# A macaron transformer in float32 on one core: the expert layers as two halves of 648 columns, with LoRA amid the next tile's product

## The chip, the cores and the metric

The kernel runs on one core of a Trainium2 chip. Its engines are TensorE (PE in the profile; its weight loads are PEld), VectorE (DVE), ScalarE (ACT), GpSimd (POOL) and SyncE (SP), which issues the DMAs. Each executes its own instructions in order and waits on semaphores for the others. The time is that of one execution on the device, in microseconds; the lower the better.

## The reference

```python
x = L0_attn_x                                    # [2, 1024, 512] float32
x = x + 0.5 * L0_ffn(layernorm(x))               # weight-normed W + lora_B @ lora_A
x = x + L0_attn(layernorm(x))                    # 32 heads of 16, 8 kv heads, rope, causal
x = x + 0.5 * L0_ffn(layernorm(x))
x = x + 0.5 * L1_ffn(layernorm(x))               # experts
x = x + L1_attn(layernorm(x))                    # 8 heads of 32, causal
x = x + 0.5 * L1_ffn(layernorm(x))
...
def L1_ffn(x, W_base, b_base, W_router, lora_A, lora_B):       # E = 8 experts, R = 16, top 2
    logits = xf @ W_router.T                                   # [tokens, 8]
    topk_p, topk_i = top_k(softmax(logits), 2)
    topk_p = topk_p / sum(topk_p)
    w = sum(one_hot(topk_i, 8) * topk_p[..., None], axis=1)
    h = einsum('td,erd->ter', xf, lora_A)                      # [tokens, 8, 16]
    lora_out = einsum('ter,eor,te->to', h, lora_B, w) * 2.0
    return x @ W_base.T + b_base + lora_out
```

## The kernel before, in words

Each of the two sequences (1024 rows of 512) goes through eight stages, numbered FFN_A, QKV0, WO0, FFN_B, MOE_A, QKV1, WO1, MOE_B. MOE_A and MOE_B are the expert layers. A stage works on eight tiles of 128 rows. Stages are joined to three chains, [FFN_A, QKV0], [WO0, FFN_B, MOE_A, QKV1] and [WO1, MOE_B], with an attention after each of the first two. In a chain a list of (stage, tile) items is run through in software-pipelined steps: at step i every engine does its share of item i, i-1, i-2 and so on. The order within a step is written out by hand, once per engine, in the function `chain` of that engine; semaphores do the rest.

For an item, GpSimd computes the inverse deviation (`rstd_of`, L1191 and L1193), VectorE the statistics (`statistics`, L803, L805) and the normalised tile xn (`normalise`, L815), TensorE transposes it into a bank called `turn` (`turn_x`, L567), ScalarE copies the high part out of it (`copy_turned`, L1051), VectorE subtracts that to get the low part (`turned_lo`, L822), and TensorE multiplies (`product`): a float32 product is made of three passes in a rounded format, high x high, high x low and low x high (`three_passes`, L587, L588, L589), over four chunks of 128 input features. The result stands in one of two pairs of PSUM banks, `prod[n % 2]`, and VectorE takes it up (`epilogue`: L847 or L850 for x, L841 for QKV). Weights of the next stage are split into high and low parts during tiles 2 to 5 of the stage before, one chunk a tile, the high part on ScalarE (L1060), the low part on GpSimd (`split_chunk`, L1184). GpSimd also adds the bias to x ahead of the update (`bias_x`, L1204).

An expert item has more. TensorE's `router` multiplies the tile by `whl`, the 128 columns of all experts' lora_A and the 8 columns of the router, 136 columns into bank 1 of the pair. VectorE's `routing` takes the two greatest logits and their places and forms two rows of gates (L864 to L873), with an exponential on ScalarE (L1066) between; each of the nine steps waits for the one before (`link`). `weigh` adds the rows (L877) and multiplies the 128 columns by them (L881, to `hw`). TensorE transposes hw (`turn_hw`, L617), ScalarE copies it out (`copy_hw`, L1071), and TensorE adds its product with lora_B to bank 0, where the base product of 512 columns stands (`lora`, L622). The bias is halved once at the start and the update multiplies the product by 0.5.

TensorE's step i is: transposes of item i, turn_hw of item i-2, router of item i-1, lora of item i-2, base product of item i-1. VectorE's is: statistics of item i+2, normalise i+1, low part of i, update of i-2, routing and weighing of i-1.

## Time and profile before

| | before |
|---|---|
| median of 3 runs | 1426.17 us |
| all three | 1425.89, 1426.17, 1436.26 us |
| the profiled execution | 1425.2 us, span of its instructions 1423.5 us |
| TensorE busy | 1298.5 us, 91% of the span, 7328 matmuls |
| VectorE busy | 963.8 us, 68%, 2846 instructions |
| ScalarE, GpSimd busy | 630.8 us (44%), 485.5 us (34%) |
| chain that ended last | PE 68%, DVE 17%, POOL 5%, issue 5%, ACT 3%, DMA 2% |
| DMA | 38.50 MB, mean 27 GB/s |

Busy times come from the profile of one execution. Matmuls overlap in it (a record lasts until the results are out), so a TensorE that is busy by the profile need not be issuing at its full rate; the time from one matmul's start to the next one's tells its cost. The clock column gives the share of full speed that TensorE was granted.

### The profile page before, as it was taken

The page shows a single profiled execution, that of the slowest core. Times are in us where ns is not written, and L with a number is a line of the kernel's source. Part 1 is how long each engine was busy: PE and PEld are TensorE (multiplying, and loading weights), DVE is VectorE, ACT ScalarE, POOL GpSimd, SP SyncE. Part 2 cuts the span into 40 slices and gives each one's busy share as a digit, 9 for nine tenths or more (in the row PEclk, how much of TensorE's full clock was granted, in tenths as well). Part 3 has the DMA queues.
Part 4 walks back from the last instruction along what each step waited for, and adds up shares of the span by engine and source line. Part 5 has one row for each costly group of instructions (what it writes and reads, how often), then busy time and mean ns, then how long its engine had stood idle before and what let it go on. Part 6 is the DMA issues. An engine that isn't in the chain of part 4 may idle for free.

```text
span 1423.5 us, 21475 instructions
## 1 busy us (share of the span) xinstructions
PE 1298.5 (91%) x7328; PEld 799.1 (56%) x7328; DVE 963.8 (68%) x2846; ACT 630.8 (44%) x929; POOL 485.5 (34%) x734
## 2 busy tenths in 40 slices
PE   4997999999899898998879889999988999999898
PEld 1875544444277686445658754444434877854366
DVE  5765898899257845644758467999871787376276
ACT  1245366666622245443212544766665222634421
POOL 1574032221255442116426621311223653311261
PEclk8999599999999998999989975999999999989999
DMA  9200000110011000000130000010100100000001
GB/s 299 88 1 30 2 2 2 32 32 3 1 35 37 1 1 30 2 1 5 55 144 1 24 8 2 3 32 2 32 3 1 56 15 1 31 2 2 1 16 45
DMA packets 19932, 38.50 MB, mean 27 GB/s; under 512 B 4416, under 2 KB 6208, under 8 KB 19712
## 3 DMA queue, kind: packets, MB, share of 16 engines
q1 hardware_dynamic: 19824, 37.12, 7.8%
q8 instruction: 60, 0.98, 0.3%
q14 instruction: 48, 0.39, 0.1%
HBM read 31.21 MB, written 11.01 MB: 30 GB/s over the span
## 4 chain that ended last, share of the span: by engine, by line
PE 68%; DVE 17%; POOL 5%; issue 5%; ACT 3%; DMA 2%; SPq 0%; DVEq 0%; ACTq 0%; POOLq 0%
PE bank L758 15%; PE bank L660 12%; PE bank L587 7%; PE bank L589 7%; PE bank L588 7%; DVE maxes L949 5%; PE bank L742 4%; PE bank L640 4%; PE bank L736 3%; DVE unused L945 3%; PE bank L567 2%; PE bank L622 2%; PE bank L670 2%; POOL probs L1221 2%; DVE x L847 1%
## 5 line engine op out<-in xcount | busy, mean ns | idle before, releaser
L1149 ACT ACTIVATE probs<-bank 128x1024 f32<-128x1024 f32 (+3 forms) x416 | 368.0, 911 | 301.5 <-PE bank L742 192.5
L660 PE MATMUL bank<-ops 48*128 48x512 f32 (+3 forms) x960 | 323.5, 441 | 13.3 <-DVE maxes L949 4.1
L945 DVE CUSTOM_DVE_ANT_0 unused<-bank,causal 128x128 bf16<-128x128 f32 (+3 forms) x640 | 279.4, 486 | 73.0 <-PE bank L660 69.8
L1301 POOL TENSOR_SCALAR_AFFINE_SELECT probs<-probs 128x256 f32<-128x256 f32 (+1 forms) x256 | 118.8, 464 | 587.6 <-ACT probs L1149 587.3
L660 PEld LDWEIGHTS bank<-ops 48*128 48x128 f32 (+1 forms) x960 | 164.2, 208 | 198.1 <-DVE maxes L945 79.6
L758 PE MATMUL bank<-probs,v_mem 128*17 128x512 f32 (+6 forms) x1920 | 256.1, 524 | 6.1 <-ACT heads_raw L1138 5.6
L949 DVE TENSOR_REDUCE maxes<-bank 128x1 f32<-128x512 f32 x320 | 207.3, 684 | 40.3 <-PE bank L660 38.8
L1051 ACT CAST xT<-bank 128x512 fp32r<-128x512 f32 (+1 forms) x128 | 71.2, 560 | 271.7 <-PE bank L567 271.7
L742 PE MATMUL bank<-ops 50*128 50x512 f32 (+2 forms) x640 | 178.5, 454 | 4.9 <-ACT probs L1149 4.8
L822 DVE TENSOR_TENSOR xT<-bank,xT 128x512 fp32r<-128x512 f32 (+1 forms) x128 | 83.5, 655 | 125.0 <-ACT xT L1051 124.9
L587 PE MATMUL bank<-w_odd_hi,xT 128*128 128x512 f32 (+1 forms) x384 | 155.4, 405 | 1.9 <-DVE xT L822 1.9
L589 PE MATMUL bank<-w_odd_hi,xT 128*128 128x512 f32 (+1 forms) x384 | 138.0, 359 | 0.0
L588 PE MATMUL bank<-w_odd_lo,xT 128*128 128x512 f32 (+1 forms) x384 | 137.7, 359 | 0.0
L742 PEld LDWEIGHTS bank<-ops 50*128 50x128 f32 x640 | 88.0, 200 | 58.2 <-ACT probs L1149 29.7
L1106 ACT CAST ops<-bank 128x512 fp32r<-128x512 f32 x144 | 81.7, 587 | 65.9 <-PE bank L640 65.7
L587 PE MATMUL bank<-ops,xT 128*128 128x512 f32 x224 | 100.3, 448 | 4.0 <-DVE x L847 1.6
L640 PE MATMUL bank<-identf,features 128*128 128x128 f32 x512 | 78.5, 290 | 19.5 <-POOL heads_raw L1258 13.9
L1191 POOL TENSOR_SCALAR var_eps<-mv 128x1 f32<-128x1 f32 x96 | 38.9, 405 | 159.1 <-DVE mv L805 158.9
L589 PE MATMUL bank<-ops,xT 128*128 128x512 f32 x224 | 90.1, 402 | 0.0
L588 PE MATMUL bank<-ops,xT 128*128 128x512 f32 x224 | 89.8, 401 | 0.0
L758 PEld LDWEIGHTS bank<-probs,v_mem 128*17 128x17 f32 (+1 forms) x1920 | 41.0, 99 | 78.0 <-issue 52.6
L640 PEld LDWEIGHTS bank<-identf,features 128*128 128x128 f32 x512 | 62.4, 147 | 37.7 <-POOL heads_raw L1258 17.3
(109 smaller groups left out, 1896.1 us busy)
## 6 DMA issues: line engine op xcount, KB each, us to landing
w_odd_lo<-staging_wqkv SPq DMA_DIRECT2D x4, 1536.0 KB, 6.7
x<-x_dram SPq DMA_DIRECT2D x16, 256.0 KB, 5.9
out_dram<-x SPq DMA_DIRECT2D x16, 256.0 KB, 2.0
staging_wqkv<-wqkv_dram SPq DMA_DIRECT2D x2, 1536.0 KB, 14.0
ops<-staging_dora SPq DMA_DIRECT2D x3, 1024.0 KB, 5.5
ops<-shiftT SPq DMA_DIRECT2D x160, 4.0 KB
w_odd_lo<-staging_wo SPq DMA_DIRECT2D x2, 1024.0 KB, 5.2
ops<-staging_base SPq DMA_DIRECT2D x2, 1024.0 KB, 5.5
```

What stands on the lines that cost most here:

```text
L587: mm(dst, x_hi[:, k, :], hi[:, k, :], start=(k == 0), stop=False)
L588: mm(dst, x_hi[:, k, :], lo[:, k, :], start=False, stop=False)
L589: last = mm(dst, x_lo[:, k, :], hi[:, k, :], start=False, stop=(k == kc - 1 and not lora))
L640: last = nc.tensor.transpose(dst[:, k * P:(k + 1) * P], src, identf[:])
L660: last = mm(dst[:, h * w:(h + 1) * w], queries(a, u)[rows, t // 4, hi, t % 4 * P:(t % 4 + 1) * P], keys(a, u, hi)[rows, HALF * kp:HALF * k ...
L742: last = mm(dst, keys(a, u, 0)[rows, block], queries(a, u)[rows, c, heads_of[0]:heads_of[-1] + 1, columns], start=True, stop=True)
L758: last = mm(heads[a.head_rows * h:a.head_rows * h + a.dim + 1, q0 - HALF * c:HALF], v[:, j, a.kv_head(u, r, i), :], probs[:, e % 6, n, fir ...
L822: V.tensor_tensor(xT[:, n % 2, 1, 0:kc, :], turn[n % 2][:, 0:kc * P].rearrange("p (k c) -> p k c", k=kc), xT[:, n % 2, 0, 0:kc, :].bitcast ...
L945: V.tensor_tensor_reduce(unused[:, masked % 3, 0:w], part, causal[:, HALF - w:], 1.0, NEG, ALU.add, ALU.max, dst).then_inc(s["max_done"].s ...
L949: V.tensor_reduce(dst, part, AX.X, ALU.max).then_inc(s["max_done"].sem, 1)
L1149: A.activation(probs[:, e % 6, :, 0:cols], scores[:, 2 * (e % 2):2 * (e % 2) + 2, 0:cols], ACT.Exp, scale=a.scale).then_inc(s["exp"].sem, 1)
L1301: G.affine_select(out=p, in_=p, compare_op=ALU.is_ge, fill=0.0, base=0, pattern=pattern, channel_multiplier=-1).then_inc(s["masked"].sem, 1)
```

## The change

The expert layers' three weight matrices (lora_A, router, base: 128 + 8 + 512 columns) become one of 648 columns, staged, loaded and split together. Each tile's product is done as two halves of 324 columns: the first holds lora_A, the router and the first 188 columns of the base, the second the other 324 columns of the base. turn_hw of the tile before comes between the halves, writing to a `turn` bank, and lora of the tile before after the second chunk of the second half; it is now two matmuls, into 188 columns of bank 1 and 324 of bank 0. The 188 base columns of the first half are added to x in `routing`, and the update has two parts. Routing is shorter: ScalarE takes the exponential of the difference of the two greatest logits by itself and copies the places, and the division by the sum moves into the weighing multiply. On VectorE the low part now comes first in every step of every chain, routing before normalise, and weighing stays last. QKV's 768 columns are multiplied as 384 + 384, before 512 + 256. The region X grows, and the base weights are loaded after unit 6 of the first attention, before after unit 5.

```diff
-        whl = sb("whl", [P, 2, KC, ER + EXPERTS], F32R)
-                   "X": [ops_flat[:, 4096:6144], ops_flat[:, 6144:8192]],
+                   "X": [ops_flat[:, 4096:7168], ops_flat[:, 7168:10240]],
...
-                    if st == QKV0 and u in (3, 5):
+                    if st == QKV0 and u in (3, 6):
...
+                st3, t3 = divmod(n - 3, NT)
+                if st3 in MOE_RANK:
+
+                    pe.wait_ge(hwT_ready.sem, hwT_ready.at(b, MOE_RANK[st3] * NT + t3 + 1))
...
-                for c in range(2 if st in ATT else 1):
-                    cols = slice(c * 512, min(hi.shape[2], (c + 1) * 512))
...
+                w = hi.shape[2] // (2 if st in ATT else 1)
+                for c in range(hi.shape[2] // w):
+                    cols = slice(c * w, (c + 1) * w)
+                    last = three_passes(prod[n % 2][:, c, 0:w], n, hi[:, :, cols], lo[:, :, cols], between=between)
+                last.then_inc(prod_ready.sem, 1)
+
+            def expert_half(b, st, t, first, between=None):
+
+                n = begin(b, st, t) if first else st * NT + t
+                if t == 0 and first:
+                    pe.wait_ge(w_ready.sem, w_ready.at(b, chunks_before(st + 1)))
+                cols = slice(0, MOE_HALF) if first else slice(MOE_HALF, MOE_COLS)
+                last = three_passes(prod[n % 2][:, 1 if first else 0, 0:MOE_HALF], n, weights(st, 0)[:, :, cols],
+                                    weights(st, 1)[:, :, cols], lora=not first, between=between)
+                if first:
+                    last.then_inc(hl_ready.sem, 1)
...
-                mm(prod[n % 2][:, 0, :], hwT[r % 2], wlora[:, :], start=False, stop=True).then_inc(prod_ready.sem, 1)
+                mm(prod[n % 2][:, 1, MOE_HALF:MOE_HALF + BASE_FIRST], hwT[r % 2], wlora[:, 0:BASE_FIRST], start=True, stop=True)
+                mm(prod[n % 2][:, 0, 0:MOE_HALF], hwT[r % 2], wlora[:, BASE_FIRST:], start=False, stop=True
+                   ).then_inc(prod_ready.sem, 1)
...
+                    if st in MOE_RANK:
+                        first, rest = x[:, t, 0:BASE_FIRST], x[:, t, BASE_FIRST:]
+                        dve.wait_ge(base_added.sem, base_added.at(b, MOE_RANK[st] * NT + t + 1))
+                        V.scalar_tensor_tensor(first, prod[n % 2][:, 1, MOE_HALF:MOE_HALF + BASE_FIRST], 0.5, first,
+                                               ALU.mult, ALU.add)
+                        V.scalar_tensor_tensor(rest, prod[n % 2][:, 0, 0:MOE_HALF], 0.5, rest, ALU.mult, ALU.add
+                                               ).then_inc(x_new.sem, 1)
...
+                V.max(top[:], logits).then_inc(route_top.sem, 1)
+                dve.wait_ge(route_top.sem, route_top.at(b, r + 1))
+                V.max_index(top_at[:], top[:], logits).then_inc(route_at.sem, 1)
+                dve.wait_ge(x_biased.sem, x_biased.at(b, BIAS_RANK[st] * NT + t + 1))
+                V.scalar_tensor_tensor(x[:, t, 0:BASE_FIRST], prod[n % 2][:, 1, ER + EXPERTS:MOE_HALF], 0.5,
+                                       x[:, t, 0:BASE_FIRST], ALU.mult, ALU.add).then_inc(base_added.sem, 1)
...
+                dve.wait_ge(route_exp.sem, route_exp.at(b, 2 * (r + 1)))
+                V.tensor_scalar(route[:, 1:2], route[:, 0:1], 1.0, 0.5, ALU.add, ALU.mult).then_inc(route_sum.sem, 1)
+                V.tensor_scalar(gate[:, 1, :], expert_no[:], top_atf[:, 1:2], route[:, 0:1], ALU.is_equal, ALU.mult
+                                ).then_inc(route_second.sem, 1)
+                dve.wait_ge(route_sum.sem, route_sum.at(b, r + 1))
+                V.reciprocal(route[:, 2:3], route[:, 1:2]).then_inc(route_inv.sem, 1)
+                dve.wait_ge(route_second.sem, route_second.at(b, r + 1))
+                V.scalar_tensor_tensor(gate[:, 0, :], expert_no[:], top_atf[:, 0:1], gate[:, 1, :], ALU.is_equal, ALU.add
+                                       ).then_inc(gate_sum.sem, 1)
...
             def chain(b, its):
                 for i in range(len(its) + 4):
+                    if i < len(its):
+                        turned_lo(b, *its[i])
                     if i + 2 < len(its):
                         statistics(b, *its[i + 2])
+                    experts = 1 <= i < len(its) + 1 and its[i - 1][0] in MOE_RANK
+                    if experts:
+                        routing(b, *its[i - 1])
                     if i + 1 < len(its):
                         normalise(b, *its[i + 1])
-                    if i < len(its):
-                        turned_lo(b, *its[i])
...
-                act.wait_ge(route_step.sem, route_step.at(b, 9 * r + 2))
-                A.activation(route[:, 1:2], route[:, 0:1], ACT.Exp).then_inc(route_exp.sem, 1)
+                act.wait_ge(route_top.sem, route_top.at(b, r + 1))
+                A.activation(route[:, 0:1], top[:, 0:1], ACT.Exp, bias=top[:, 1:2], scale=-1.0).then_inc(route_exp.sem, 1)
+                act.wait_ge(route_at.sem, route_at.at(b, r + 1))
+                A.copy(top_atf[:], top_at[:, 0:2]).then_inc(route_exp.sem, 1)
```

VectorE in the middle of MOE_A, before. A row is a line of the kernel, the operation, what it writes and reads, its partitions x elements, and the semaphores that it waits for. `top` and `top_at` are the greatest logits and their places, `gate` the gates, `hw_mem` the weighed activations.

```order
L803 BN_STATS stats<-x 128x6 [waits x_new]
L805 BN_AGGR mv<-stats 128x2 [waits ln_stat]
L815 TENSOR_SCALAR probs<-x,mv,rstd 128x512 [waits turned,ln_rstd]
L822 TENSOR_TENSOR xT<-bank,xT 128x512 [waits xT_hi_ready]
L847 SCALAR_TENSOR_TENSOR x<-bank,x 128x512 [waits x_biased,prod_ready]
L864 MAX top<-bank 128x8 [waits hl_ready]
L865 TENSOR_TENSOR route<-top 128x1 [waits route_step]
L866 MAX_INDEX top_at<-top,bank 128x8 [waits route_step]
L867 CAST top_atf<-top_at 128x2 [waits route_step]
```

The same place now (the kernel's lines have other numbers: L844 is the low part, L837 normalise, L887 to L891 routing, L872 and L874 the update, L898 to L910 weighing):

```order
L904 SCALAR_TENSOR_TENSOR gate<-expert_no,top_atf,gate 128x8 [waits route_second]
L910 SCALAR_TENSOR_TENSOR hw_mem<-bank,route,gate 128x128 [waits gate_sum,route_inv]
L844 TENSOR_TENSOR xT<-bank,xT 128x512 [waits xT_hi_ready]
L825 BN_STATS stats<-x 128x6 [waits x_new]
L827 BN_AGGR mv<-stats 128x2 [waits ln_stat]
L887 MAX top<-bank 128x8 [waits hl_ready]
L889 MAX_INDEX top_at<-top,bank 128x8 [waits route_top]
L891 SCALAR_TENSOR_TENSOR x<-bank,x 128x188 [waits x_biased]
L837 TENSOR_SCALAR probs<-x,mv,rstd 128x512 [waits turned,ln_rstd]
L872 SCALAR_TENSOR_TENSOR x<-bank,x 128x188 [waits base_added,x_biased,prod_ready]
L898 TENSOR_SCALAR route<-route 128x1 [waits route_exp]
L899 TENSOR_SCALAR gate<-expert_no,top_atf,route 128x8
```

The low part moved from behind normalise to the head of the step, routing from behind the update to ahead of normalise, and the weighing alone stays behind the update.

TensorE in the middle of MOE_A, before, from the transposes of one tile to its first base matmuls (the router's twelve rows cut to three):

```order
L567 MATMUL bank<-identf,probs 128x128 [waits xT_ready,xn_ready]
L617 MATMUL bank<-identf,hw_mem 128x128 [waits hw_ready]
L587 MATMUL bank<-whl,xT 128x136 [waits x_new,xT_ready]
L588 MATMUL bank<-whl,xT 128x136
L589 MATMUL bank<-whl,xT 128x136
L622 MATMUL bank<-wlora,hw_mem 128x512 [waits hwT_ready]
L587 MATMUL bank<-ops,xT 128x512
```

And now (L576 is the transposes, L596 to L598 the three passes, L629 turn_hw, L634 and L635 lora):

```order
L576 MATMUL bank<-identf,probs 128x128 [waits hwT_ready,xT_ready,xn_ready]
L596 MATMUL bank<-ops,xT 128x324 [waits x_new,xT_ready]
L597 MATMUL bank<-ops,xT 128x324
L598 MATMUL bank<-ops,xT 128x324
L629 MATMUL bank<-identf,hw_mem 128x128 [waits hw_ready]
L596 MATMUL bank<-ops,xT 128x324
L634 MATMUL bank<-wlora,hw_mem 128x188 [waits hwT_ready]
L635 MATMUL bank<-wlora,hw_mem 128x324
```

turn_hw moved from ahead of the router to behind a whole half product, and lora from ahead of the base product to six matmuls into its second half.

## Rows read from the trace of the kernel before

**Rows 1.** Windows: length; busy of PE, PEld, DVE, ACT, POOL; clock; DMA share, GB/s.

```profile
444.50:503.70 59.20, 54.04 (x293) 42.55 (x292) 46.94 (x148) 12.15 (x30) 29.34 (x40) 1.00 0.03 10
670.50:734.60 64.10, 51.00 (x255) 38.80 (x255) 44.76 (x141) 10.31 (x28) 24.19 (x31) 0.91 0.20 69
1367.70:1423.50 55.80, 49.41 (x254) 37.59 (x254) 38.92 (x135) 7.95 (x24) 17.78 (x22) 0.96 0.10 38
478.40:485.23 6.83, 5.72 (x32) 4.46 (x31) 5.54 (x22) 1.05 (x3) 2.25 (x3) 1.00 0.00 0
485.23:491.06 5.83, 5.71 (x32) 4.46 (x31) 4.68 (x18) 0.96 (x3) 2.25 (x3) 1.00 0.01 3
428.44:431.65 3.21, 3.21 (x17) 2.65 (x16) 2.54 (x6) 1.11 (x2) 2.30 (x3) 1.00 0.13 53
```

**Rows 2.** Timeline, an expert tile: start, us, engine, line, operation, out and in.

```profile
473.51 0.28 PE L588 MATMUL bank<-whl,xT 128*128 128x136 f32 x1
...
474.12 0.44 POOL L1191 TENSOR_SCALAR var_eps<-mv 128x1 f32<-128x1 f32 x1 [2.69 <-DVE mv L805]
...
474.74 1.07 PE L622 MATMUL bank<-wlora,hw_mem 128*128 128x512 f32 x2
475.18 1.83 POOL L1184 TENSOR_TENSOR w_odd_lo<-w_odd_lo,w_odd_hi 128x768 fp32r<-128x768 f32 x1
...
475.85 0.69 DVE L847 SCALAR_TENSOR_TENSOR x<-bank,x 128x512 f32<-128x512 f32 x1 [0.77 <-PE bank L622]
475.88 0.39 PE L588 MATMUL bank<-ops,xT 128*128 128x512 f32 x1
...
476.11 0.40 PE L589 MATMUL bank<-ops,xT 128*128 128x512 f32 x1
...
476.97 1.29 POOL L1204 TENSOR_TENSOR x<-x,bbase 128x512 f32<-128x512 f32 x1
...
477.34 0.94 DVE L867 CAST top_atf<-top_at 128x2 f32<-128x2 uint32 x1
...
480.11 0.33 PE L617 MATMUL bank<-identf,hw_mem 128*128 128x128 f32 x1 [1.11 <-DVE hw_mem L881]
```

**Rows 3.** Group by line and shape, VectorE: busy us, mean ns, idle before.

```profile
L881 DVE TENSOR_TENSOR hw_mem<-bank,gate 128x128 f32<-128x128 f32 x32 | 9.3, 291 | 1.3 <-DVE gate L877 0.3
```

**Rows 4.** Timeline, TensorE in a QKV0 tile, 256 columns.

```profile
73.02 0.28 PE L587 MATMUL bank<-w_odd_hi,xT 128*128 128x256 f32 x1
73.14 0.28 PE L588 MATMUL bank<-w_odd_lo,xT 128*128 128x256 f32 x1
```

**Rows 5.** Timeline in the first attention, VectorE and GpSimd.

```profile
195.54 0.67 DVE L985 TENSOR_SCALAR shifts<-maxes 128x16 fp32r<-128x16 f32 x1
195.54 0.64 POOL L1301 TENSOR_SCALAR_AFFINE_SELECT probs<-probs 128x512 f32<-128x512 f32 x1
196.14 1.27 POOL L1184 TENSOR_TENSOR w_odd_lo<-w_odd_lo,w_odd_hi 128x512 fp32r<-128x512 f32 x1
196.24 1.20 DVE L987 SCALAR_TENSOR_TENSOR shifts<-maxes,shifts 128x16 fp32r<-128x16 f32 x1
```

**Rows 6.** Timeline, an FFN_B tile whose transposes start at 428.44.

```profile
429.08 0.59 ACT L1051 CAST xT<-bank 128x512 fp32r<-128x512 f32 x1 [2.09 <-PE bank L567]
...
429.69 0.69 DVE L822 TENSOR_TENSOR xT<-bank,xT 128x512 fp32r<-128x512 f32 x1 [0.64 <-ACT xT L1051]
...
430.30 0.68 DVE L850 TENSOR_TENSOR x<-bank,x 128x512 f32<-128x512 f32 x1
...
430.90 0.68 DVE L803 BATCH_NORM_STATS2 stats<-x 128x6 f32<-128x512 f32 x1
...
431.72 0.53 DVE L815 TENSOR_SCALAR probs<-x,mv,rstd 128x512 f32<-128x512 f32 x1
```

**Rows 7.** Timeline, TensorE at the start of the second batch.

```profile
734.56 1.11 PE L567 MATMUL bank<-identf,probs 128*128 128x128 f32 x4 [6.38 <-DVE probs L815]
...
737.08 0.79 PE L587 MATMUL bank<-ops,xT 128*128 128x512 f32 x1
```

More of the change, by code:

```diff
@@ L42 @@
 NEG = -1e30
+MOE_COLS = ER + EXPERTS + D
+MOE_HALF = MOE_COLS // 2
+BASE_FIRST = MOE_HALF - ER - EXPERTS
 SHIFT_DELAY = 3
@@ L372, in build @@
         s_eff = {n: ctx.enter_context(nc.semaphore(f"eff_{n}")) for n in
-                 ("ab", "sum", "sq", "norm", "sqrt", "inv", "scale", "ready", "half_bias", "router_parts")}
+                 ("ab", "sum", "sq", "norm", "sqrt", "inv", "scale", "ready", "half_bias")}
         w_loaded = [signal(f"w_loaded{st}", 16) for st in range(8)]
@@ L685, in chain, with lora_between @@
                         turn_x(b, *its[i])
+                    experts = 1 <= i < len(its) + 1 and its[i - 1][0] in MOE_RANK
+                    if experts:
+                        expert_half(b, *its[i - 1], True)
                     if 2 <= i < len(its) + 2 and its[i - 2][0] in MOE_RANK:
                         turn_hw(b, *its[i - 2])
-                    if 1 <= i < len(its) + 1 and its[i - 1][0] in MOE_RANK:
-                        router(b, *its[i - 1])
-                    if 2 <= i < len(its) + 2 and its[i - 2][0] in MOE_RANK:
+                    if experts:
+                        chunk = [0]
+                        def lora_between():
+                            chunk[0] += 1
+                            if chunk[0] == 2 and i >= 2 and its[i - 2][0] in MOE_RANK:
+                                lora(b, *its[i - 2])
+                        expert_half(b, *its[i - 1], False, between=lora_between)
+                    elif 2 <= i < len(its) + 2 and its[i - 2][0] in MOE_RANK:
                         lora(b, *its[i - 2])
@@ L699, in next_piece @@
                             turn_piece(b, st, t, todo.pop(0))
-                    if 1 <= i < len(its) + 1:
+                    if 1 <= i < len(its) + 1 and not experts:
                         product(b, *its[i - 1], between=next_piece)
@@ L923, in chain @@
                             rope_cos_part(b, *its[i - 2])
-                    if 1 <= i < len(its) + 1 and its[i - 1][0] in MOE_RANK:
-                        routing(b, *its[i - 1])
+                    if experts:
                         weigh(b, *its[i - 1])
@@ L1215, in rope @@
                     pool.wait_ge(s["roped"].sem, s["roped"].at(b, t))
+                if b == 0 and t == 0:
+                    pool.wait_ge(s_early, 16 * 2)
                 for im in range(2):
```

77 lines of the change are left out of this document (24 added, 53 removed).

## The prediction

> **What bounds the kernel now.** I read the windows of the four expert stages first, then one expert tile in the timeline, then a tile of the stages around it. The windows [rows 1] show, in their first three rows, that MOE_A with the start of QKV1 costs 59.2 us (its twin in the second batch 59.1), and MOE_B 64.1 in the first batch and 55.8 us in the second: 238.2 us together, one sixth of the span. One expert tile takes 6.83 us while the next stage's weights are being split and 5.83 us when they are not, and in both TensorE is busy for 5.7. The FFN tile takes 3.21 us with TensorE full.
>
> The timeline [rows 2] shows what the expert tile waits for, a ring through four engines. From the start of VectorE's update of x (L847, 475.85) to the transpose of the weighed activations (L617, 480.11) is 4.26 us: the update and nine routing steps, each waiting for the one before. Then TensorE does that transpose and the 12 router matmuls, at 0.112 us each (11 of them from 473.51 to 474.74), 1.46 in all, then LoRA, and 1.11 us after LoRA's start the next update begins. 4.26 + 1.46 + 1.11 = 6.83. TensorE's remaining work is base and transposes, which lie beside the routing. The clock is 1.00 in these tiles. So the expert tile is bound by this ring, not by TensorE.
>
> **TensorE's part.** Base matmuls of 512 columns follow each other at 0.23 us [rows 2], those of 256 at 0.12 [rows 4]. At the full clock (2.4 GHz) 512 and 256 columns stream in 0.213 and 0.107 us, so about 14 ns per matmul comes on top, and I put 324 columns at 0.149 and 384 at 0.174. QKV: 0.228 + 0.120 = 0.348 us per chunk and pass before, 2 x 0.174 now: nothing, 32 tiles long. Expert: 12 x (0.228 + 0.112) = 4.08 us before, 24 x 0.149 = 3.58 now. Transposes of x are 3.21 - 12 x 0.228 = 0.47 [rows 1], the small transpose 0.10, LoRA 0.91 (474.74 to the base stream that ends 0.23 before 475.88); two LoRA matmuls with the same 512 columns in all, 0.92. An expert tile on TensorE: 0.47 + 3.58 + 0.10 + 0.92 = 5.07 us.
>
> The Trainium skill (TensorE: Matmul & The Clock Gate, Back-to-back issue gap) gives N / 2.4 + 2.5 ns for a warm matmul standing alone. By it 24 matmuls of 324 columns would take 3.30 us and the expert tile 4.79, some 8 us less over the tiles; the rows of this case stand above it (0.23 against its 0.216), so the sum goes by the rows.
>
> **The ring that is cut.** Routing now starts after the first half, and the update of the tile before no longer stands between router and routing. The ring left is transpose to LoRA (six matmuls, 0.9), LoRA 0.92, about 0.2 to its end, both updates, and the weighing: 0.1 + 0.9 + 0.92 + 0.2 + 0.8 + 1.4 = 4.3 us, below TensorE's 5.07. ScalarE's copy and the exponential fit beside the six matmuls.
>
> **VectorE, next in line.** From FFN rows [rows 6]: low part to next operation 0.61, statistics to normalise 0.82 when adjacent. Update of 512 columns 0.69 us, the weighing multiply of 128 columns 0.29 [rows 3]: 1.04 ns per column and 0.16 fixed, so 188 columns 0.35 and 324 columns 0.50, of which some 0.08 overlaps the next. In the new order, from the start of the low part: statistics 0.61, their aggregate 1.33, max 1.43, index 1.63, first base update 1.91, normalise 2.18, two updates 2.63 and 2.90, then the weighing at 3.32: sum, gate, reciprocal, gate sum, multiply, some 1.15 us (the multiply 0.29 [rows 3], the four smaller ones bounded by the same and put at 0.2). 4.5 us: hidden below 5.07, if nothing holds it up.
>
> GpSimd does. In [rows 5] a tensor_scalar of 16 columns takes 0.67 us and a scalar_tensor_tensor of 16 columns 1.20, and each ends where a GpSimd operation ends (196.18, 197.41); in [rows 2] L867 takes 0.94, ending with L1204. Operations with PSUM as an input, like L847, keep 0.69. The new weighing has three operations of the blocked kinds (L898, L899, L904 of the new order) just where GpSimd works: its long operation starts 1.06 us after L1191 begins [rows 2], sooner (about 0.85) when normalise doesn't hold L1191 back, so at 2.5, and normalise, waiting from 2.18, goes in between and pushes it to 2.9. Without a split, the bias addition (1.29) ends at 4.1, the weighing's first operation ends with it instead of at 3.4, and the tile takes 5.1: level with TensorE. With a 768-column split (1.83) GpSimd is busy until 4.6 and then adds the bias until 5.9; the first operation ends with the split, the gate or gate sum with the bias, the multiply follows, and the low part of the next tile starts between 6.2 and 6.6. I take 6.4. With a 512-column split it is 5.6 to 6.0, I take 5.8. The slack between the engines takes up 0.7 once per stage.
>
> The Trainium skill (SBUF — State Buffer, Who interferes with whom) says that issue order decides who blocks, the first holding the ports throughout; by it the two gates would pass if they came ahead of the bias, and a split tile would be near 5.2. L867 came after L1204 in the rows; the new order has not been seen. That is the first rival.
>
> **The sum over the expert stages.** Middle stages, before 59.2: 3.2 (FFN's last product, as now) + 4.05 (first product, no LoRA) + 3 x 5.1 + 4 x 6.4 - 0.7 + 7.1 = 54.6. The 7.1 is the first tile after the stage: TensorE has no expert half to do and waits for the last weighing, then transpose, copy and LoRA stand alone before QKV's 4.18; bounds 6.4 and 7.8. Saved 4.6, twice 9.2. Last stage of the first batch: 3.7 + 4.1 + 4 x 5.8 - 0.7 + 5.1 + a tail of 18.6 (20.2 now, less 1.6 in the last tile) = 54.0 against 64.1; its clock was 0.91 [rows 1] and a cold stretch may come back, so I count 9.1. Last stage of the second batch, no splits: 3.7 + 4.1 + 5 x 5.1 + 15.9 = 49.2 against 55.8, 6.6. Together 24.9.
>
> **What the new order costs elsewhere.** The low part is now ahead of statistics and normalise in every stage. FFN tile [rows 6, 1]: the transposes start at 428.44, the high part at +0.64, the low part at +1.25. Before, normalise stood ahead of it. Now it follows: 1.25 + 0.61 + 0.82 = 2.68, done 3.21, next transposes at 3.27 against 3.21. The update follows at 3.13 and ends 3.81, the product after it may start at 3.87, and 3.87 + 2.73 = 6.6 for two tiles gives 3.30. So 0.09 for each of 28 FFN tiles: 2.6 us, bounds 0 and 6. At each batch's start TensorE waits on the same order. Second batch [rows 7]: first transposes 734.56, first product 737.08; now normalise of the second tile ends 3.7 to 3.8 us after the first transposes (cold clock), the product starts near 739.1, 2.0 later. First batch 0.6. Together 5.2.
>
> At nothing: the dropped load, copy and subtraction of the small weights at the start lie beside the weight-norm matmuls; the wider splits (648 columns, +0.27 us on GpSimd, +0.1 on ScalarE, four per stage) lie in FFN tiles where GpSimd has 0.9 of 3.2 free; the later base load, now 1.3 MB, waits behind unit 6 in SP's queue, with unit 7's shifts behind it, and has over 100 us. If SP held those shifts for the whole transfer it would be 7 us a batch; nothing in the trace points to it.
>
> 24.9 - 5.2 = 19.7. The profiled execution took 1425.2 us, giving 1405.5; the median of the runs is 1.0 higher: **1406 us**. A measurement here tells about 1% (14 us) from no change.
>
> **Rivals.** (1) VectorE's gates slip in ahead of GpSimd's operations: eight split tiles 1.2 us less and four 0.6 less, 12 us more gained, 1394. For it: the operations are tiny and issued without a wait between. Against: every L867 that met L1204 was held. 0.25. (2) The hold is worse: both gates wait whole bias additions, tiles without a split come to 5.6, with one to 6.9, and FFN tiles take 3.4. Of the 24 full expert iterations 12 have a split and 12 don't: 24 x 0.5 + 28 x 0.1 = 15 less, a gain of 5, 1421. 0.13. (3) Slower: a matmul of 324 or 384 columns isn't proportional. No such width exists before; the nearest rows are 512 and 256. If each cost what 512 do, 0.228, QKV tiles would rise by 24 x 0.054 = 1.3 and expert tiles reach 24 x 0.228 + 1.49 = 6.96, against 6.83 and 5.83: 32 x 1.3 + 12 x 0.1 + 12 x 1.1 + 5.2 for the order = 61, 1487. It turns the change into a loss from 15 ns more per matmul (56 tiles x 24 x 15 ns = 20 us). Against: the 14 ns on top is the same at two widths. 0.05. (4) The ring isn't what bounds and nothing moves: speaks against it that 4.26 + 1.46 + 1.11 closes at the period. 0.02.
>
> **How the numbers follow.** Forecast 0.55 (1399 to 1412), rival 1 0.25, rival 2 0.13, rival 3 0.05, rival 4 0.02. The range for 8 in 10 takes the forecast, nearly all of rival 1 and the near part of rival 2: 1391 to 1417. Faster by over 1% (below 1412) is 0.53 + 0.25 = 0.78; within 1% is 0.13 + 0.02 + 0.02 = 0.17; slower 0.05.
>
> **What would show it.** Right: expert tiles of 5.1 us where no split runs, with VectorE and TensorE both above 4.5 busy; 6.2 to 6.6 where a 768 split runs, L899 or L904 ending with a bias addition; FFN tiles of 3.3; QKV tiles still 4.62. Wrong would be expert matmuls not 0.15 apart, a weighing that no GpSimd operation stretches, or FFN tiles above 3.5.

## The result and the profile after

The changed kernel takes 1409.55 us (median of 4 runs, 1405.42 to 1412.15), the kernel before 1430.91 beside it (4 runs, 1425.89 to 1436.26): a ratio of 0.985 [0.982, 0.989], 1.5% faster. The forecast was 1406 us with a range of 1391 to 1417. The profiled execution has a span of 1409.8 us and took 1411.57; before it was 1423.5 and 1425.2. The granted clock was 0.929 on average, before 0.933.

The windows of the kernel after, each cut from the start of one stage to the start of another as in [rows 1]: first MOE_A with two steps of QKV1, then MOE_B of each batch, then an expert tile beside a 768-column split, one without a split, and an FFN tile. The columns are those of [rows 1].

```profile
448.50:501.08 52.58, 49.57 (x309) 45.75 (x309) 44.84 (x131) 14.67 (x38) 27.23 (x39) 1.00 0.03 11
671.72:724.51 52.79, 43.62 (x271) 39.29 (x271) 39.49 (x123) 12.32 (x36) 23.16 (x31) 0.94 0.25 85
1360.75:1409.82 49.07, 43.98 (x270) 40.45 (x270) 33.96 (x118) 10.13 (x32) 16.80 (x23) 0.95 0.12 44
...
478.29:484.21 5.92, 5.25 (x36) 4.81 (x34) 5.75 (x16) 1.32 (x4) 3.86 (x5) 1.00 0.00 0
1378.82:1383.82 5.00, 5.00 (x36) 4.81 (x34) 4.11 (x17) 1.32 (x4) 2.04 (x3) 1.00 0.14 52
431.57:434.90 3.33, 3.33 (x18) 2.60 (x17) 2.37 (x6) 1.22 (x2) 2.46 (x3) 1.00 0.02 7
```

The stages of [rows 1] went from 59.20, 64.10 and 55.80 us to 52.58, 52.79 and 49.07. The tile without a split went from 5.83 to 5.00 with TensorE (the second number) busy in all of it; the tile with one from 6.83 to 5.92, where TensorE has 0.67 to spare and VectorE and GpSimd together set the pace. The FFN tile rose from 3.21 to 3.33. A split, here and below, is GpSimd's subtraction (L1215) that makes the low part of a chunk of the next stage's weights.

The timeline of the kernel after shows how, in that split tile (VectorE and GpSimd, with TensorE's small transpose):

```profile
475.32 0.68 DVE L844 TENSOR_TENSOR xT<-bank,xT 128x512 fp32r<-128x512 f32 x1
...
476.64 0.18 DVE L827 BATCH_NORM_AGGREGATE mv<-stats 128x2 f32<-128x6 f32 x1
...
477.21 0.68 POOL L1224 TENSOR_TENSOR rstd<-var_eps,minus_half 128x1 f32<-128x1 f32 x1
477.33 0.54 DVE L837 TENSOR_SCALAR probs<-x,mv,rstd 128x512 f32<-128x512 f32 x1
477.75 1.84 POOL L1215 TENSOR_TENSOR w_odd_lo<-w_odd_lo,w_odd_hi 128x768 fp32r<-128x768 f32 x1
...
478.45 0.14 DVE L898 TENSOR_SCALAR route<-route 128x1 f32<-128x1 f32 x1
478.51 1.11 DVE L899 TENSOR_SCALAR gate<-expert_no,top_atf,route 128x8 f32<-128x8 f32 x1
...
479.54 1.30 POOL L1235 TENSOR_TENSOR x<-x,bbase 128x512 f32<-128x512 f32 x1
479.65 1.21 DVE L904 SCALAR_TENSOR_TENSOR gate<-expert_no,top_atf,gate 128x8 f32<-128x8 f32 x1
480.96 0.35 DVE L910 SCALAR_TENSOR_TENSOR hw_mem<-bank,route,gate 128x128 f32<-128x128 f32 x1
481.23 0.68 DVE L844 TENSOR_TENSOR xT<-bank,xT 128x512 fp32r<-128x512 f32 x1
481.37 0.33 PE L629 MATMUL bank<-identf,hw_mem 128*128 128x128 f32 x1 [0.67 <-DVE hw_mem L910]
...
482.54 0.18 DVE L827 BATCH_NORM_AGGREGATE mv<-stats 128x2 f32<-128x6 f32 x1
```

L899 works on eight columns and takes 1.11 us, ending (479.62) as the split L1215 ends (479.59). L904 takes 1.21 and ends (480.86) as the bias addition L1235 ends (480.84). The period closes as a ring over two engines: aggregate 476.64, inverse root, split, bias addition, gate sum, multiply 480.96, low part 481.23, statistics, aggregate 482.54, which is 5.90 us. Where no split runs the same two operations are short, and the low part follows sooner:

```profile
1378.79 0.14 DVE L898 TENSOR_SCALAR route<-route 128x1 f32<-128x1 f32 x1
...
1378.85 0.28 DVE L899 TENSOR_SCALAR gate<-expert_no,top_atf,route 128x8 f32<-128x8 f32 x1
...
1379.16 0.23 DVE L904 SCALAR_TENSOR_TENSOR gate<-expert_no,top_atf,gate 128x8 f32<-128x8 f32 x1
...
1379.71 0.31 PE L596 MATMUL bank<-w_odd_hi,xT 128*128 128x324 f32 x1
1379.86 0.31 PE L597 MATMUL bank<-w_odd_lo,xT 128*128 128x324 f32 x1
1380.01 0.31 PE L598 MATMUL bank<-w_odd_hi,xT 128*128 128x324 f32 x1
...
1383.11 0.35 DVE L872 SCALAR_TENSOR_TENSOR x<-bank,x 128x188 f32<-128x188 f32 x1 [0.49 <-PE bank L635]
```

The matmuls of 324 columns start 0.15 apart. VectorE now waits for TensorE (the last row), where TensorE waited for VectorE in [rows 2].

The FFN tile, timeline of the kernel after, answering to [rows 6]:

```profile
431.57 0.60 PE L576 MATMUL bank<-identf,probs 128*128 128x128 f32 x4
...
432.82 0.69 DVE L844 TENSOR_TENSOR xT<-bank,xT 128x512 fp32r<-128x512 f32 x1 [0.92 <-ACT xT L1080]
433.43 0.68 DVE L825 BATCH_NORM_STATS2 stats<-x 128x6 f32<-128x512 f32 x1
...
434.25 0.53 DVE L837 TENSOR_SCALAR probs<-x,mv,rstd 128x512 f32<-128x512 f32 x1
...
434.69 0.68 DVE L879 TENSOR_TENSOR x<-bank,x 128x512 f32<-128x512 f32 x1
434.90 0.60 PE L576 MATMUL bank<-identf,probs 128*128 128x128 f32 x4
```

VectorE waits 0.92 us for the transposed tile with nothing else to do, since statistics and normalise stand behind it now. The transposes of the next tile start 0.65 after normalise starts, and the period is 3.33.

To see where the whole went I added up the steps, from each stage's first transposes to the next stage's, for both profiled executions:

| part | before | after | difference |
|---|---|---|---|
| four expert stages | 213.1 | 183.2 | -29.9 |
| four FFN stages | 114.5 | 121.4 | +6.9 |
| both WO1 | 33.3 | 35.8 | +2.5 |
| QKV0, step from tile 5 to 6, both batches | 22.8 | 27.5 | +4.7 |
| rest (startup, QKV, attention, WO0) | 1039.8 | 1041.9 | +2.1 |
| span | 1423.5 | 1409.8 | -13.7 |

### The profile page after: what moved, and what is told of

Its sections match the earlier page's. It is cut to its first block, busy times and chain, and to the rows that moved or that the text cites. A ratio compares the mean times of both kernels' runs of the same rounds, so it can differ in the third digit from the quotient of the medians.

```text
span 1409.8 us, 21535 instructions
## 1 busy us (share of the span) xinstructions
PE 1286.9 (91%) x7392; PEld 824.5 (58%) x7392; DVE 943.4 (67%) x2782; ACT 639.8 (45%) x959; POOL 483.3 (34%) x733
## 4 chain that ended last, share of the span: by engine, by line
PE 69%; DVE 16%; POOL 5%; issue 4%; ACT 4%; DMA 2%; SPq 0%; DVEq 0%; ACTq 0%; POOLq 0%
PE bank L781 16%; PE bank L674 12%; PE bank L596 8%; PE bank L598 7%; PE bank L597 7%; DVE maxes L980 5%; PE bank L765 4%; PE bank L654 4%; PE bank L759 3%; PE bank L576 3%; DVE unused L976 3%; PE bank L684 2%; POOL probs L1254 1%; DVE xT L844 1%; DVE gate L904 1%
## 5 line engine op out<-in xcount | busy, mean ns | idle before, releaser
L781 PE MATMUL bank<-probs,v_mem 128*17 128x512 f32 (+6 forms) x1920 | 259.1, 531 | 6.1 <-ACT heads_raw L1169 5.6
L844 DVE TENSOR_TENSOR xT<-bank,xT 128x512 fp32r<-128x512 f32 (+1 forms) x128 | 83.6, 656 | 148.4 <-ACT xT L1080 148.4
L596 PE MATMUL bank<-w_odd_hi,xT 128*128 128x384 f32 (+2 forms) x448 | 169.0, 377 | 2.1 <-DVE xT L844 1.9
L598 PE MATMUL bank<-w_odd_hi,xT 128*128 128x384 f32 (+2 forms) x448 | 152.8, 341 | 0.0
L597 PE MATMUL bank<-w_odd_lo,xT 128*128 128x384 f32 (+2 forms) x448 | 152.6, 341 | 0.0
L596 PE MATMUL bank<-ops,xT 128*128 128x512 f32 (+1 forms) x288 | 114.3, 397 | 5.3 <-DVE x L877 3.4
L1222 POOL TENSOR_SCALAR var_eps<-mv 128x1 f32<-128x1 f32 x96 | 34.8, 363 | 202.3 <-DVE mv L827 202.3
L598 PE MATMUL bank<-ops,xT 128*128 128x512 f32 (+1 forms) x288 | 104.0, 361 | 0.0
L597 PE MATMUL bank<-ops,xT 128*128 128x512 f32 (+1 forms) x288 | 103.7, 360 | 0.0
L596 PEld LDWEIGHTS bank<-w_odd_hi,xT 128*128 128x128 f32 x448 | 85.8, 192 | 7.7 <-DVE xT L844 2.4
L597 PEld LDWEIGHTS bank<-w_odd_lo,xT 128*128 128x128 f32 x448 | 86.0, 192 | 3.5
```

Of the source, the lines that this page charges most:

```text
L596: mm(dst, x_hi[:, k, :], hi[:, k, :], start=(k == 0), stop=False)
L597: mm(dst, x_hi[:, k, :], lo[:, k, :], start=False, stop=False)
L598: last = mm(dst, x_lo[:, k, :], hi[:, k, :], start=False, stop=(k == kc - 1 and not lora))
L781: last = mm(heads[a.head_rows * h:a.head_rows * h + a.dim + 1, q0 - HALF * c:HALF], v[:, j, a.kv_head(u, r, i), :], probs[:, e % 6, n, fir ...
L844: V.tensor_tensor(xT[:, n % 2, 1, 0:kc, :], turn[n % 2][:, 0:kc * P].rearrange("p (k c) -> p k c", k=kc), xT[:, n % 2, 0, 0:kc, :].bitcast ...
```

## The experiments

A step is timed from the first transpose of one tile's x to the next one's. "Expert stages" and "FFN stages" are the sums of the table, of each run's profiled execution. Ratios are to the kernel before, timed beside the run: 1428.69 us beside the first four, 1426.28 beside the last three; the three between were executed once each.

**VectorE's order put back where no expert tile is in the pipeline.** From the kernel after; the low part stays first only in steps with an expert item.

```diff
-                    if i < len(its):
+                    experts = 1 <= i < len(its) + 1 and its[i - 1][0] in MOE_RANK
+                    if experts and i < len(its):
                         turned_lo(b, *its[i])
...
                         normalise(b, *its[i + 1])
+                    if not experts and i < len(its):
+                        turned_lo(b, *its[i])
```

> The changed kernel, but with VectorE's old order (statistics, normalise, low part) in every step that has no expert item; expert steps keep the new order. If the low part's place is what lengthens the other stages: FFN tiles back from 3.27 to 3.53 to 3.21 us, the QKV0 step of 13.7 us back to about 11.4, the second batch's first FFN tile from 3.8 to about 1.3, in all 12 to 15 us off the changed kernel (near 1395). Rival, that the even halves of QKV or the wider splits of 648 columns lengthen them: these tiles stay as they are and the time is within 3 us of the changed kernel. Expert tiles stay at 5.0, 5.35 and 5.9 us in both.

1400.39 us (1396.38 to 1404.41, 4 runs), 0.981 [0.978, 0.984] of the kernel before. Expert stages 183.1 us as in the kernel after, FFN stages 114.1 against 121.4, and the second batch's first step again 1.27 us (3.78 in the kernel after). The rival, that the halves or the wider splits lengthen the FFN tiles, is gone by that. Two numbers were missed: the QKV0 step fell only to 12.7, not to 11.4, and the kernel came out 9 us below the kernel after by the medians, not 12 to 15. The windows row of FFN_B:

```profile
414.47:440.10 25.63, 25.63 (x129) 21.15 (x128) 20.16 (x41) 7.23 (x12) 14.13 (x20) 1.00 0.21 77
```

That is 25.63 us for eight steps, TensorE full, where the kernel after takes 27.27. So the order costs 7.3 us in the FFN stages (1.5 of it in the first batch's FFN_A, whose early steps differ by more than that among runs of one order), 0.4 in one step of each QKV1 (6.83 against 6.40) and 1.0 in one of each QKV0: 10 us in all. The expert stages take the same time, so they don't need it outside their own steps. By the medians it is 9 us, but the intervals of the two ratios overlap, so the size rests on the stages.

**The order alone.** From the kernel before.

```diff
                 for i in range(len(its) + 4):
+                    if i < len(its):
+                        turned_lo(b, *its[i])
                     if i + 2 < len(its):
                         statistics(b, *its[i + 2])
                     if i + 1 < len(its):
                         normalise(b, *its[i + 1])
-                    if i < len(its):
-                        turned_lo(b, *its[i])
```

> The kernel before with one edit: VectorE's low part ahead of statistics and normalise in every step. If the place of the low part is the cause: FFN tiles of 3.3 to 3.5 us, the QKV0 step near 13.7, and 10 to 15 us slower than before; expert tiles unchanged at 5.8 and 6.8, since there the ring of routing sets them. Rival (halves or wider splits are the cause): FFN tiles 3.21, no difference from before.

1471.8 us (1467.11 to 1480.4, 4 runs), 1.032 [1.028, 1.035]: 43 us slower, where 10 to 15 were expected and the expert tiles should have stayed as they were. The FFN stages are as foreseen (122.3). The rest is in the expert stages, 241.1 us against 213.1, with single tiles of 11.3 us. The windows of the second MOE_A and of one such tile, and then the timeline in it:

```profile
1161.86:1221.14 59.28, 52.02 (x232) 40.63 (x232) 41.43 (x117) 10.22 (x25) 25.66 (x29) 0.83 0.03 10
1184.00:1195.40 11.40, 9.08 (x36) 6.82 (x35) 8.21 (x21) 1.78 (x4) 7.86 (x8) 0.78 0.00 0
```

```profile
1185.38 1.63 DVE L865 TENSOR_TENSOR route<-top 128x1 f32<-128x1 f32 x1
...
1187.32 0.92 DVE L867 CAST top_atf<-top_at 128x2 f32<-128x2 uint32 x1
...
1190.05 0.33 PE L617 MATMUL bank<-identf,hw_mem 128*128 128x128 f32 x1 [2.32 <-DVE hw_mem L881]
...
1192.46 2.01 PE L622 MATMUL bank<-wlora,hw_mem 128*128 128x512 f32 x2
...
1194.51 0.69 DVE L847 SCALAR_TENSOR_TENSOR x<-bank,x 128x512 f32<-128x512 f32 x1 [2.65 <-PE bank L622]
```

With nothing between normalise and the update, the old routing starts as GpSimd starts its split: L865, one column wide, takes 1.63 us, and L867 0.92. TensorE idles 2.32 us. Then its clock falls: the stage's mean is 0.83 against 1.00 for MOE_A in [rows 1], and the LoRA matmuls take 2.01 us against 1.07 in [rows 2]. Beside the short routing the same order stands in expert stages of 183.2 us; beside the long one it makes them 28 us longer than before. It can't be taken over by itself.

**The gates out of GpSimd's reach.** From the kernel after: the expert numbers are copied into an unused PSUM bank once per stage, and the second gate row is written there.

```diff
-                V.tensor_scalar(gate[:, 1, :], expert_no[:], top_atf[:, 1:2], route[:, 0:1], ALU.is_equal, ALU.mult
+                V.tensor_scalar(ps_gate, ps_no, top_atf[:, 1:2], route[:, 0:1], ALU.is_equal, ALU.mult
...
-                V.scalar_tensor_tensor(gate[:, 0, :], expert_no[:], top_atf[:, 0:1], gate[:, 1, :], ALU.is_equal, ALU.add
+                V.scalar_tensor_tensor(gate[:, 0, :], expert_no[:], top_atf[:, 0:1], ps_gate, ALU.is_equal, ALU.add
```

> The changed kernel with the expert numbers and the second gate row held in a free PSUM bank, so that the two gate operations (tensor_scalar and scalar_tensor_tensor) have at most one SBUF tensor as an input each. If GpSimd's split and bias addition hold them through what they share in SBUF: the two no longer take 1.1 and 1.2 us beside them but 0.3, the 5.90 us tiles fall to 5.0 to 5.3 and the 5.35 ones to 5.0, 6 to 9 us off the changed kernel. Rival (these tiles are long because VectorE or GpSimd has too much to do in them, whoever holds whom): they stay above 5.7 and the gain is under 2 us.

Tiles came out as expected: every full expert tile takes 5.00 us, with a split or without. VectorE's groups by line and shape, first of the kernel after, then of this one (busy us, mean ns):

```profile
L899 DVE TENSOR_SCALAR gate<-expert_no,top_atf,route 128x8 f32<-128x8 f32 x32 | 19.6, 613 | 0.0
L904 DVE SCALAR_TENSOR_TENSOR gate<-expert_no,top_atf,gate 128x8 f32<-128x8 f32 x32 | 18.1, 565 | 0.0
```

```profile
L904 DVE TENSOR_SCALAR bank<-bank,top_atf,route 128x8 f32<-128x8 f32 x32 | 9.1, 285 | 0.0
L909 DVE SCALAR_TENSOR_TENSOR gate<-expert_no,top_atf,bank 128x8 f32<-128x8 f32 x32 | 7.1, 222 | 0.0
```

The two operations fall from 613 and 565 ns to 285 and 222, and the expert stages to 176.0 us, 7.2 less. So the hold of these two operations made the split tile 5.9 us, and not the amount of work, since VectorE and GpSimd have the same operations to do but for one small copy a stage: the rival is refuted. The total does not show it: 1409.63 us (1402.33 to 1413.81, 4 runs), 0.985 [0.982, 0.989], the same as the kernel after. What took most of it back in the profiled execution stands in the windows of the second batch's first attention, in the kernel after and in this one:

```profile
796.31:1088.52 292.21, 272.11 (x1725) 126.94 (x1724) 221.22 (x739) 176.50 (x221) 72.99 (x124) 0.89 0.04 14
```

```profile
786.74:1087.43 300.69, 282.60 (x1725) 131.67 (x1724) 222.46 (x739) 177.24 (x221) 73.08 (x124) 0.85 0.04 13
```

The same instructions, the same work of VectorE and ScalarE to 1%, but a clock of 0.85 instead of 0.89, and 8.5 us more. The first batch's went the other way, 288.1 us at 0.92 against 292.0 at 0.89. Nothing in the edit touches that stage. Over the whole program the clock was 0.921 to 0.931 in the four runs here and 0.927 to 0.934 in the four of the kernel after, so the missing gain goes with a lower clock; why the clock is lower no run here shows.

The Trainium skill (SBUF — State Buffer, Who interferes with whom) says that a VectorE instruction with at most one input in SBUF doesn't contend with GpSimd outside the two-port modes, and one with two such inputs does. By it L904 of the kernel after (expert numbers and gates both in SBUF) is held and L909 here (gates in PSUM) is not; the trace agrees, 565 against 222 ns. L899 has only one tensor in SBUF as an input and was held too, 613 ns against 285 with its tensors in PSUM; what sets it apart no run here settles.

**Both together.** The order of the first experiment and the gates of the third.

> Both edits at once, old order outside the expert steps and the gates in PSUM. If the two causes are separate the gains add: 18 to 24 us off the changed kernel, near 1388, all full expert tiles near 5.0 and FFN tiles 3.21. If one gives back what the other takes (a stage that starts earlier meets a later transfer, or the clock drops), less than 15.

1392.82 us (1384.8 to 1402.59, 6 runs), 0.975 [0.971, 0.979]. Expert stages 175.9, FFN stages 113.5. Against the kernel after it is 1.1% by the ratios, 16.7 us by the medians, a little under the 18 to 24 expected. The interval is clear of that of the kernel after, but not of that of the first experiment.

**QKV columns as 512 and 256 again.** From the kernel after.

```diff
-                w = hi.shape[2] // (2 if st in ATT else 1)
-                for c in range(hi.shape[2] // w):
-                    cols = slice(c * w, (c + 1) * w)
+                for c in range(2 if st in ATT else 1):
+                    cols = slice(c * 512, min(hi.shape[2], (c + 1) * 512))
```

> The changed kernel with QKV's 768 columns as 512 + 256 again. If a matmul costs its columns at the clock plus a fixed 14 ns, nothing moves: QKV tiles of 4.61 to 4.63 us as in the changed kernel and in the one before. Rival (two even halves cost more, or less, than an uneven pair, for instance through the weight load that each matmul has beside it): tiles off by 0.1 us or more.

One run: 1400.8 us. QKV steps of 4.61 to 4.63, as with even halves and as before. The cost of 384 columns lies in line with those of 512 and 256, and the even halves neither cost nor give anything in these steps. One run can't place the total: single runs of the kernel after lie 7 us apart.

**LoRA ahead of the second half.** From the kernel after: lora follows turn_hw at once, not after six more matmuls.

```diff
-                            if chunk[0] == 2 and i >= 2 and its[i - 2][0] in MOE_RANK:
-                                lora(b, *its[i - 2])
+                        if i >= 2 and its[i - 2][0] in MOE_RANK:
+                            lora(b, *its[i - 2])
```

> The changed kernel with LoRA straight behind the transpose of the weighed activations, ahead of the second half instead of two chunks into it. If those six matmuls are what covers ScalarE's copy: TensorE waits 0.5 to 0.7 us for it in every tile, MOE_B tiles of the second batch 5.5 to 5.7 us instead of 5.0, those with a 768-column split stay near 5.9, since VectorE sets them. Rival (the place of LoRA doesn't matter once it is behind the first half): 5.0.

1415.59 us, one run. A tile without a split takes 5.61 us instead of 5.00, with TensorE 5.25 busy (windows, then timeline in that tile):

```profile
1386.55:1392.16 5.61, 5.25 (x35) 4.81 (x33) 4.21 (x15) 1.32 (x4) 2.67 (x4) 1.00 0.14 51
```

```profile
1389.08 0.27 ACT L1102 COPY hw_mem<-bank 128x128 f32<-128x128 f32 x1 [1.30 <-PE bank L629]
...
1389.40 0.59 PE L634 MATMUL bank<-wlora,hw_mem 128*128 128x188 f32 x2 [0.35 <-ACT hw_mem L1102]
```

TensorE waits in each tile from its small transpose to ScalarE's copy of it. The expert steps of MOE_A are 5.71, 5.61, 5.65, 5.89 and 5.92, against 5.06, 5.36, 5.90, 5.90 and 5.92 in the kernel after. The last ones stay at 5.9, so the two limits don't add: the hold hides this wait. Six matmuls between are worth 0.6 us in each tile that isn't held, as expected.

**The shorter routing alone.** From the kernel before: only routing, weighing and ScalarE's exponential and copy of the two places are those of the kernel after (code in the diff ahead of the prediction); router, LoRA, base and the order stay.

> The kernel before with only the shorter routing (exponential straight from the two logits and the copy of the places on ScalarE, division moved into the weighing multiply); router, base, LoRA and the order of the steps as before. If the ring of update, routing, router and LoRA sets the tile, it shrinks by the steps taken out, some 0.5 to 0.9 us, until TensorE's 5.6 stops it: tiles without a split from 5.8 to 5.6, those with one from 6.8 to 5.8 to 6.3. That would be at most half of what the whole change gained; the rest needs the new places of router, update and LoRA. Rival (the shorter routing alone is the gain): 5.0 to 5.3.

1398.8 us, one run; expert stages 192.5 against 213.1. That is 20.6 of the whole change's 29.9 us: not at most half, as I had expected, but two thirds. A tile without a split takes 5.51 us, with TensorE busy in all of it: the old work (0.47 + 4.08 + 0.10 + 0.91 = 5.56 by the prediction's terms) had been the second limit, just 0.3 below the ring. A tile with a 768-column split takes 5.91, with TensorE at 5.73:

```profile
457.00:462.90 5.90, 5.73 (x34) 4.54 (x32) 4.05 (x14) 1.95 (x6) 4.08 (x5) 1.00 0.01 1
```

**The same, timed.** Same kernel.

> The kernel before with the shorter routing alone, as in the look before, now timed: full expert tiles of 5.51 us without a split and 5.91 with one, expert stages 192 to 193 us in all; by the tiles 20 us below the kernel before, ratio 0.984 to 0.988. Rival (the one look owed its time to the clock in the attentions): 0.99 or more.

1404.95 us (1401.78 to 1407.4, 4 runs), 0.985 [0.982, 0.989]. The tiles are as foreseen and the total lies in the expected range, so the gain wasn't the clock's. The shorter routing alone is worth as much as the whole change. The rest of the change gains 9 us more in the expert stages and gives it back, most of it through the order and 2.5 us in WO1.

**The shorter routing with the gates in PSUM.** From the kernel before: the routing of the last two runs with the gates of the third experiment.

> The kernel before with the shorter routing and the gates in PSUM. Here TensorE's own work fills 5.51 us of the tile, and only the tiles with a 768-column split stand above that, so the gates' freedom gives back 0.4 us in 8 tiles and 0.2 in 4: expert stages 188 to 190 us, 3 to 4 us below the shorter routing alone. If what holds the split tiles here is not the gates but normalise, they stay at 5.9.

1409.89 us (1404.35 to 1413.11, 4 runs), 0.989 [0.986, 0.993]: no gain, and the expectation failed. The gates had hardly been stretched here, 344 and 227 ns on average without this edit against 285 and 223 with it, and a split tile stays at 5.91. The timeline shows another chain ahead of LoRA:

```profile
468.17 0.84 ACT L1065 CAST w_odd_hi<-w_odd_lo 128x768 fp32r<-128x768 f32 x1
...
468.90 0.27 ACT L1078 COPY hw_mem<-bank 128x128 f32<-128x128 f32 x1
...
469.22 1.13 PE L628 MATMUL bank<-wlora,hw_mem 128*128 128x512 f32 x2 [0.17 <-ACT hw_mem L1078]
...
470.38 0.69 DVE L853 SCALAR_TENSOR_TENSOR x<-bank,x 128x512 f32<-128x512 f32 x1 [1.39 <-PE bank L628]
```

ScalarE's cast of the next weights stands ahead of its copy of the weighed activations, the copy releases LoRA, and LoRA the update. With TensorE within 0.2 us of full it has no slack for that. This is read from the timeline; no run takes the cast away. In the kernel after, LoRA comes behind six matmuls and the copy is off this path, and there the hold of the gates is what sets a split tile, as the third experiment shows. The median 5 us above the run before it isn't explained by the stages (190.8 against 191.8 in the expert stages); in the profiled execution the second batch's first attention took 298.1 us against 291.5, at a clock of 0.86 against 0.89. For the other runs of the two kernels that is open.

**The best version again.**

> The changed kernel with VectorE's old order outside the expert steps and the gates in PSUM, timed beside the two above. By the tiles (expert stages 176 us, FFN stages 113.5) it should lie 12 to 14 us below the kernel before with shorter gates, less some 3 us for the wider splits in WO1: ratio to the kernel before 0.970 to 0.978. If the halves give back elsewhere what they gain in the expert stages, the three come out within 4 us of each other.

1393.8 us (1387.72 to 1406.36, 8 runs), 0.975 [0.972, 0.978]. The gain of both edits repeats on another chip. Its profiled execution was the slowest of the eight, at a clock of 0.911 with 300.8 us or more in each first attention, and yet its expert stages are those of the first run (175.6 us), and its FFN stages too (114.9 against 113.5) except early steps of the first FFN_A.

## Why the prediction was right

The time was within 4 us of the forecast and the mechanism is the one forecast, but two terms were off in opposite directions, and that they partly cancelled is luck. So is part of the nearness itself: the profiled spans moved by 13.7 us where 19.7 was forecast, and the medians by 21.4, with the four runs of the kernel before spread over 10 us.

**The ring, and TensorE behind it: right.** Forecast 5.07 us for a tile without a split, measured 5.00, TensorE full. 324-column matmuls 0.149 forecast, 0.15 measured; two LoRA matmuls 0.92 forecast, 0.86 measured (1382.05 to 1383.06, less the 0.15 of a base matmul). Rival 4 is gone by that, rival 3 by the 0.15 and by the QKV steps, unchanged at 4.62 as forecast and no different in 512 and 256.

**The hold by GpSimd: right in kind, too dear in size.** Forecast 6.4 us with a 768-column split, measured 5.36 in the first such tile of a stage and 5.90 in three; forecast 5.8 with a 512-column split, measured 5.00 in the first and 5.35 in three. Two steps of it failed. I let the bias addition or the split start late, because normalise would push the inverse root by 0.4; it did not, and the split starts 2.43 us after the low part instead of 2.9. And I called L898 a held operation; with one column it ran in 0.14 us in the middle of a split. The expected order of the other two, L899 to the end of the split and L904 to the end of the bias addition, is what the trace shows, and taking their operands out of SBUF gave all tiles 5.00. Rival 1, the gates slipping through, is refuted by the same rows. GpSimd's operation had started first both times, 477.75 ahead of 478.51 and 479.54 ahead of 479.65. The Trainium skill (SBUF — State Buffer, Who interferes with whom) lets issue order decide, and by that order the trace agrees with it; the 5.2 us rested on the gates coming first, which they don't. Rival 2's tiles of 5.6 and 6.9 did not come either, though its FFN tiles of 3.4 did.

**The sum over the expert stages: 24.9 forecast, 31.2 measured** in the same windows (238.2 to 207.0, the second MOE_A with its two QKV1 steps at 52.57). Middle stages 52.6 against 54.6, last stage of the first batch 52.8 against 55.0, of the second 49.1 against 49.2. Of the 6.3 missed, 5.7 lies in the full tiles of the three stages with splits, most of it in the split tiles, and 1.0 is the allowance for a cold stretch in the first batch's MOE_B; the rest nearly cancels.

**The order of VectorE: 5.2 forecast, 6.9 measured in the FFN stages, and more outside.** The step after normalise was put at 3.27 and measured 3.33, the update at 3.13 against 3.12; but over FFN_B the mean step is 3.41 and not 3.30. The start of the second batch costs 2.5 where 2.0 was said. The two QKV1 steps add 0.8, and the wait in the two QKV0 steps below 2.0; neither was in a term.

**At nothing: one item failed.** The wider splits do not all lie in FFN tiles. For MOE_B they lie in WO1, whose steps take 1.6 to 1.9 us; there a 648-column split (1.58) and the bias addition (1.30) fill GpSimd, and VectorE's update waits for it, as the timeline of the kernel after shows:

```profile
662.47 1.31 POOL L1235 TENSOR_TENSOR x<-x,bo 128x512 f32<-128x512 f32 x1
663.72 1.57 POOL L1215 TENSOR_TENSOR w_odd_lo<-w_odd_lo,w_odd_hi 128x648 fp32r<-128x648 f32 x1
663.88 0.69 DVE L877 TENSOR_TENSOR x<-bank,x 128x512 f32<-128x512 f32 x1 [0.91 <-POOL x L1235]
```

The last two steps rise from 1.91 to 2.62 and from 4.97 to 5.53, 1.27 per batch; the first experiment keeps this with the old order, so it isn't the order. Every kernel here with splits of 648 columns takes 17.9 us or more in WO1, every one with 512 columns 16.6 to 16.7; no run changes the width alone. The cover I had named, 0.9 of 3.2 us free on GpSimd, was that of another stage.

The later load of the base weights shows none of the 7 us a batch that was feared: the first attentions take 292.0 and 292.2 us, before 292.4 and 289.6.

The QKV0 step from tile 5 to 6 was in no term. It rose from 11.4 to 13.7 us in the profiled execution, but it runs from 9.8 (the shorter routing, second batch) to 13.8 among the kernels. The fourth experiment and its repetition are one program, and have 9.98 and 11.50 in the first batch. The windows of that step, first of the kernel after, then of the fourth experiment:

```profile
83.00:96.70 13.70, 9.78 (x50) 9.07 (x49) 5.54 (x9) 5.04 (x9) 10.64 (x13) 0.75 0.00 0
```

```profile
81.30:91.30 10.00, 7.09 (x50) 6.57 (x48) 5.62 (x9) 4.32 (x7) 9.39 (x11) 1.00 0.00 0
```

The clock is 0.75 in one and 1.00 in the other; in the kernel before it is 0.85. TensorE waits in this step for GpSimd's low parts of the heads. The wait is 2.7 us in the kernel before, 2.9 in the first and fourth experiments, which have the old order and the even halves of QKV, 3.7 with the new order and no even halves (second and fifth experiment), and 3.9 with both. So of the rise of 2.3 us per batch 1.0 goes with the order and 0.2 with the even halves. The rest follows the clock, and why the clock differs in this step is open.

**The sum in the end.** Without the expert windows the forecast had +5.2; the measured span has +17.5 (31.2 less 13.7): 6.9 in FFN stages, 2.5 in WO1, 4.7 in that QKV0 step, 0.8 in QKV1's, and some 2.5 elsewhere, which no run here explains. A gain larger by 6 and a cost larger by 12 gave 6 less than forecast in the span, 13.7 for 19.7.

## What to carry to other kernels

When a chain of small operations bounds a tile, shorten the chain first and look at what the next engine's own work is: here the shorter routing alone brought 20.6 of 29.9 us. Rearranging the matmuls brought the rest, in the tiles without a split by lowering TensorE's work from 5.5 to 5.0. A reordering that one stage needs should stay in that stage; carried through the whole program it cost 9 us by the medians and ate what the second half of the change had gained. A small operation of VectorE on the critical path can last to the end of the GpSimd operation that it meets. An operand in PSUM was a cheap way out here, but it gains only where nothing else (in the kernel with the old matmuls, ScalarE's cast by the timeline) sets the same tile.

## What the hardware did that I had not expected

- Beside the same GpSimd tensor_tensor, a tensor_scalar of one column took 0.14 us (L898, 478.45) and one of eight columns 1.11 (L899, 478.51). A tensor_tensor of one column with both inputs in SBUF, beside such a split, took 1.63 (L865 of the second experiment).
- In MOE_A, whose clock was 1.00 in the other profiles that I read there, the second experiment's second MOE_A has an idle stretch of 2.3 us in every second tile, a mean clock of 0.83, and tiles of 11.3 us there where the kernel before has 6.8. In the tile shown the matmuls go at half their pace from 0.5 us behind the idle stretch on. A wait on TensorE can cost twice, once as idle time and once as clock.
- The first attention takes 288.1 to 300.9 us with the same instructions, at mean clocks of 0.92 to 0.85. In all twelve profiled executions the length goes by the clock: 288 to 290 us at 0.91 to 0.92, 290 to 293 at 0.89 to 0.90, 294.5 at 0.88, 298.1 at 0.86, 300.8 at 0.85. This spread of more than 10 us is as large as what one edit gives here, and can hide 7 us that the split tiles show from a median of four runs.
